# W1's first group loaded through ScalarE's DMA queue, and x's first total moved behind the first fp32 products

## The chip, the cores and the metric

The kernel runs on one core of one Trainium2 chip. A time is the device time of one launch in microseconds (us). The kernel before takes 1239.53 us, the median of 3 runs (1239.34 to 1239.58).

## What is computed

The inputs are x (16 batches, 512 rows, 512 columns, fp32), a list of one expert number for each batch, and the weights of two layers.

```python
h = gelu(einsum('bni,ih->bnh', x, W1) + b1)             # W1: 512 x 2048
shared_x = einsum('bnh,ho->bno', h, W2) + b2            # W2: 2048 x 384
expert_x = einsum('bnh,bhp->bnp', h, We[indices]) + be[indices][:, None, :]   # 128 columns
out = x + concatenate([shared_x, expert_x], axis=-1)
```

The gelu is the exact one. Operands and result are fp32.

## The kernel before

The kernel is written by hand for each engine: every engine runs a fixed list of instructions, and semaphores order them against each other. An fp32 product is made of three fp16 products. Each operand is scaled by a power of two and split into a high part (ScalarE, `hi`) and a low part (VectorE, `lo`); TensorE adds up hi x hi, lo x hi and hi x lo. The power of two comes from the largest absolute value of the operand: VectorE reduces each partition to its maximum, TensorE sums these over the partitions with a matmul against ones (`total`), and VectorE turns the sum into a scale with three small operations (`power`).

The 2048 hidden columns are cut into D = 4 groups (d = 0 to 3) of C = 4 tiles (c = 0 to 3) of 128. Batches 1 to 15 use Strassen-like sums of blocks. Batch 0 is plain, and it has a special start: its group 0 (d = 0) isn't split at all. `first_group` multiplies raw fp32 W1 with raw fp32 x, so that TensorE can begin as soon as the data are there, before any scale is known. Each such product of 128x128 by 128x512 in fp32 shows as two matmul records of the profile. The loops of `first_group` run over the four row blocks k of x (outside) and the four tiles c (inside), each c into a bank of its own, `banks` for c = 0 and 1, `q_ps` for c = 2, `out_ps` for c = 3. Ahead of k = 0 it waits for x's first half and for the first half of W1's group 0; ahead of k = 2 for the second halves, and there it also makes `w1_total(0, 2)`, which waits until VectorE has reduced W1's groups 0 and 1.

What each engine does at the start, in order:

- SyncE issues all loads on its one DMA queue: x's two halves of 512 KB (L356), W1's group 0 in two halves of 512 KB (L360, L361), W1's group 1 (1 MB, L303), b1, W1's groups 2 and 3, and three parts of W2.
- ScalarE loads its activation table, runs a one-column gelu (`gelu_warm`, L622), waits for x's scale, then makes the high parts of x (four `first_x_split`, L412) and of W1's group 1 (L433).
- VectorE sets `ones`; reduces x's four blocks (`first_x_top`, L671: blocks 0 and 1 need x's first half, 2 and 3 the second); makes x's scale (`first_x_scale`, L739 to L681); reduces W1's group 0 (`w1_top(0)`, L671); makes two low parts of x (L685); reduces W1's group 1 (`w1_top(1)`); two more low parts of x; then group 1's scale and so on.
- TensorE runs 36 small matmuls on `ones` (WARM, L1322), then x's total (L1270), which waits for all four of x's reductions, and then `first_group` (L1132). After it come groups 1 to 3 in the split form (L1118 to L1120), starting with `first_layer1(1, 0)`.

The scale of x isn't used by `first_group` itself; it is used by the splits that follow.

Of the kernel before, what the change touches and what calls it, by code (L numbers as in the profile page):

```python
# [19 lines left out]
KC = IN // P  # L20
# [7 lines left out]
BLOCK = KH * 2 * P  # L28
# [43 lines left out]
def build(nc, x, idx, w1, w1f, w2, w2p, we, b1, b2, be, out):  # L72
    with ExitStack() as ctx:
        def sb(name, shape, dt):
            return ctx.enter_context(nc.sbuf_tensor(name, shape, dt))

        def sem(name):
            return ctx.enter_context(nc.semaphore(name))
# [29 lines left out]
        first_x_max = sb("first_x_max", [P, KC], BF16)  # L108
# [29 lines left out]
        w1_tops, w2_tops, first_x_tops = tops[:, 0:D], tops[:, D:2 * D], tops[:, 2 * D:2 * D + KC]  # L138
# [4 lines left out]
        w1_loaded = [sem(f"w1_loaded{d}") for d in range(D)]  # L143
        w1_rest_loaded = sem("w1_rest_loaded")
# [9 lines left out]
        first_x_max_done = sem("first_x_max_done")  # L154
        first_x_all_done = sem("first_x_all_done")
# [60 lines left out]
        def place(r, part):  # L216

            return h_ring[:, r, part].rearrange("p a n -> p (a n)").bitcast(F32)

        def w1_raw(d):  # L220

            if d == 2:
                return x_raw[:, 1].rearrange("p k n -> p (k n)")
            if d == 3:
                return t_sum[:, :, :, :].rearrange("p a k n -> p (a k n)")
            return place(d, 1)
# [25 lines left out]
        def first_bank(n):  # L252

            if n % RING == 3:
                return out_ps[:, 0]
            bank = banks[:, n % RING] if n % RING < 2 else q_ps[:, 2]
            return bank.rearrange("p j n -> p (j n)")
# [39 lines left out]
        def _(sp):  # L297
# [4 lines left out]
            def load_w1(d):  # L302
                sp.dma_start(w1_raw(d), w1[d]).then_inc(w1_loaded[d], 16)  # L303
# [51 lines left out]
            for k in range(2):  # L355
                sp.dma_start(x_raw[:, 0, KH * k:KH * (k + 1)], x[0, :, KH * k:KH * (k + 1)]  # L356
                             ).then_inc(first_x_loaded[k], 16)

            half = 2 * BLOCK
            sp.dma_start(w1_raw(0)[:, :half], w1f[:, :half]).then_inc(w1_loaded[0], 16)  # L360
            sp.dma_start(w1_raw(0)[:, half:], w1f[:, half:]).then_inc(w1_rest_loaded, 16)  # L361
            load_w1(1)
            sp.dma_start(b1_sb[:, :], b1).then_inc(b1_loaded, 16)
            load_w1(2)
# [44 lines left out]
        def _(act):  # L409
# [5 lines left out]
            def x_split(b, par, i):  # L415
                if i in T_OF:
                    act.wait_ge(t_added, 4 * (b - 1) + T_READY[i])

                if isinstance(b, int) and b == 1:
                    act.wait_ge(first_l1_done, HT)  # L420
                else:
                    act.wait_ge(l1_done, OPS * (strassen(b, 0) - 1) + i + 1)
                act.wait_ge(x_scaled, b + 1)
                nc.scalar.activation(x_hi[:, i], x_operand(par, i), ACT.Copy,
                                     scale=scale[:, par, 0:1]).then_inc(x_hi_done, 1)
# [126 lines left out]
            def batch(b, par, last=False, sums=False, w2_s=False):  # L552
# [64 lines left out]
                if isinstance(b, int) and b == 1:  # L617
                    x_split(b + 1, 1 - par, P4)
                    x_split(b + 1, 1 - par, P3)

            act.wait_ge(ones_set, 1)
            nc.scalar.activation(gelu_warm[:, :], ones[:, 0:1], ACT.Gelu)  # L622
            for k in range(KC):
# [491 lines left out]
        def _(pe):  # L1115
# [6 lines left out]
            def first_group():  # L1122

                raw = w1_raw(0).rearrange("p (k c m) -> p k c m", k=KC, c=C)
                for k in range(KC):
                    if k % KH == 0:
                        pe.wait_ge(first_x_loaded[k // KH], 16)
                        pe.wait_ge(w1_loaded[0] if k == 0 else w1_rest_loaded, 16)
                    if k == KH:
                        w1_total(0, 2)  # L1130
                    for c in range(C):
                        last = nc.tensor.matmul(first_bank(c), raw[:, k, c], x_raw[:, 0, k],  # L1132
                                                start=k == 0, stop=k == KC - 1)
                        if k == KC - 1:
                            last.then_inc(first_l1_done, 1)

            def first_layer1(d, c):

                n, i, j = C * d + c, c // 2, c % 2
                if d == 1 and j == 0:  # L1140
                    pe.wait_ge(w1_lo_done, i + 1)
                elif c == 0:
                    pe.wait_ge(w1_lo_done, d + 1)
                pe.wait_ge(first_gelu_done, n - RING + 1)
                for k in range(KC):
                    if n == C:
                        pe.wait_ge(first_x_lo, k + 1)
                    op, kc = A_OP[i][k // KH], k % KH
                    last = product(first_bank(n), w1_hi[:, d, op, kc, j],
                                   w1_lo[:, d, op, kc, j], first_x[0][:, k], first_x[1][:, k], k == 0, k == KC - 1)  # L1150
                last.then_inc(first_l1_done, 1)
# [116 lines left out]
            def total(to, of, start=True):  # L1268

                return nc.tensor.matmul(to, ones[:, :P], of, start=start, stop=True, skip_group_check=True)  # L1270

            def w1_total(a, n):
                pe.wait_ge(w1_max_done, a + n)
                total(w1_tops[:, a:a + n], w_max[:, a:a + n]).then_inc(w1_all_done, n)
# [23 lines left out]
            def first_batch():  # L1298
                first_group()
                for c in range(C):  # L1300
                    first_layer1(1, c)
                    if c == 0:

                        x_total(0)
                        w1_total(2, 2)
                for c in range(C):
                    first_layer1(2, c)
                pe.wait_ge(w2_max_done, D)
                total(w2_tops, w_max[:, D:2 * D]).then_inc(w2_all_done, 1)
                for c in range(C):  # L1310
                    first_layer1(3, c)
                    if c == 1:
                        e_total(0)
                for unit in range(OT * C):
                    layer2(0, 0, unit)
                x_total(1)
                for unit in range(OT * C):
                    layer2(0, 1, unit)

            pe.wait_ge(ones_set, 1)  # L1320
            for _ in range(WARM):
                nc.tensor.matmul(out_ps[:, 1, :N // 2], ones[:, :P], ones[:, :], start=True, stop=True)  # L1322
            pe.wait_ge(first_x_max_done, KC)
            total(first_x_tops, first_x_max[:, :]).then_inc(first_x_all_done, 1)
            first_batch()
            for b in (1, 2):
                for d in range(D):
# [58 lines left out]
```

## Time and profile before

| | us |
|---|---|
| median of 3 runs | 1239.53 |
| the profiled execution, its own time | 1239.52 |
| its span, first to last instruction | 1237.8 |
| TensorE busy | 1232.1 (x9368 matmuls) |
| VectorE busy | 940.0 |
| ScalarE busy | 742.4 |

All times in the rows below count from the start of the span. The span is 1.7 us shorter than the execution's own time; what lies around it isn't in the trace. An engine's idle time in front of an instruction is given in brackets with what released the instruction. A DMA appears twice: as the short instruction that issues it (SPq, SyncE's queue) and as its time from issue to landing. A matmul's end is modelled, so neighbouring matmuls overlap in the rows; the distance between starts is what one costs.

### The profile page before, as it was taken

Reading aid. Unit: us, or ns where it says so; the run is one execution under the profiler, and the core shown is the slowest. Engines: PE = TensorE matmul, PEld = TensorE weight load, DVE = VectorE, ACT = ScalarE, POOL = GpSimd, SP = SyncE. Lnnn points to the kernel's source line nnn. Section 1 sums busy time; section 2 is a strip of 40 time slices with the busy share of each in tenths; the row PEclk is TensorE's granted clock in tenths of the full one; section 3 lists DMA queues with packets and bytes.
Section 4 is the critical chain, followed back from the end, with each engine's and each line's share of the span. In section 5 each row is a group of like instructions: output and inputs, shape, how many; then the busy total and the mean of one; then the engine's idle time right before and its main releaser. Section 6 shows DMA issues by size and latency. Waiting matters only on the chain.

```text
span 1237.8 us, 23794 instructions
## 1 busy us (share of the span) xinstructions
PE 1232.1 (100%) x9368; PEld 917.4 (74%) x9368; DVE 940.0 (76%) x1201; ACT 742.4 (60%) x944; POOL 0.2 (0%) x4
## 2 busy tenths in 40 slices
PE   9999999999999999999999999999999999999998
PEld 4456667787787777777777877778778777777775
DVE  7986677877777877768878688787787777777765
ACT  4656556666566665666566566565666656666553
POOL 0000000000000000000000000000000000000000
PEclk9999999999999999999999999999999999999999
DMA  8223123012020110202002020030300203011000
GB/s 306 69 73 123 43 77 95 1 35 69 0 102 0 54 47 0 102 0 68 34 0 102 0 96 6 0 101 0 102 0 21 81 0 102 0 51 51 1 35 35
DMA packets 25234, 64.45 MB, mean 52 GB/s; under 512 B 5104, under 2 KB 5104, under 8 KB 22000
## 3 DMA queue, kind: packets, MB, share of 16 engines
q1 hardware_dynamic: 25200, 63.99, 15.1%
q8 instruction: 22, 0.36, 0.1%
q14 instruction: 12, 0.10, 0.0%
HBM read 47.20 MB, written 16.78 MB: 52 GB/s over the span
## 4 chain that ended last, share of the span: by engine, by line
PE 99%; DMA 1%; DVE 0%; SPq 0%; issue 0%
PE banks L1118 15%; PE banks L1119 15%; PE banks L1120 15%; PE out_ps L1120 9%; PE out_ps L1119 9%; PE out_ps L1118 9%; PE q_ps L1118 8%; PE q_ps L1119 8%; PE q_ps L1120 8%; PE banks L1132 1%; DMA h_ring<-w1f_dram 1%; PE out_ps L1132 0%; PE q_ps L1132 0%; SPq L356 0%; DVE x_raw L918 0%
## 5 line engine op out<-in xcount | busy, mean ns | idle before, releaser
L1120 PE MATMUL banks<-x_hi,w_lo 128*128 128x256 f16 (+1 forms) x1704 | 467.0, 274 | 0.0
L1119 PE MATMUL banks<-x_lo,w_hi 128*128 128x256 f16 (+1 forms) x1704 | 467.0, 274 | 0.0
L1118 PE MATMUL banks<-x_hi,w_hi 128*128 128x256 f16 (+1 forms) x1704 | 467.0, 274 | 0.0
L685 DVE SCALAR_TENSOR_TENSOR h_ring<-u,scale,h_ring 128x2048 f16<-128x2048 f32 x120 | 281.1, 2343 | 6.9 <-ACT h_ring L450 4.8
L517 ACT ACTIVATE kept<-banks 128x512 f32<-128x512 f32 x180 | 106.3, 591 | 170.3 <-PE banks L1120 170.3
L1118 PEld LDWEIGHTS banks<-x_hi,w_hi 128*128 128x128 f16 x1704 | 166.7, 98 | 44.1 <-ACT kept L517 0.5
L1119 PEld LDWEIGHTS banks<-x_lo,w_hi 128*128 128x128 f16 x1704 | 166.7, 98 | 43.2 <-issue 0.3
L1120 PEld LDWEIGHTS banks<-x_hi,w_lo 128*128 128x128 f16 x1704 | 166.7, 98 | 21.8
L458 ACT ACTIVATE h_ring<-u,scale 128x2048 f16<-128x2048 f32 x56 | 112.1, 2002 | 96.7 <-DVE u L861 96.7
L548 ACT ACTIVATE u<-u,b_sb,undo 128x512 f32<-128x512 f32 x120 | 91.2, 807 | 124.1 <-DVE u L906 124.1
L893 DVE TENSOR_TENSOR u<-banks,kept 128x512 f32<-128x512 f32 x60 | 41.5, 691 | 160.5 <-PE banks L1120 148.9
L450 ACT ACTIVATE h_ring<-u,scale 128x2048 f16<-128x2048 f32 x64 | 127.5, 1992 | 4.4 <-PE out_ps L1120 4.3
L1120 PE MATMUL q_ps<-h_ring,w_sums 128*128 128x256 f16 x448 | 122.1, 273 | 0.0
L1119 PE MATMUL q_ps<-h_ring,w_sums 128*128 128x256 f16 x448 | 122.1, 272 | 0.0
L1118 PE MATMUL q_ps<-h_ring,w_sums 128*128 128x256 f16 x448 | 122.1, 272 | 0.0
L1119 PE MATMUL q_ps<-h_ring,w_hi 128*128 128x256 f16 (+1 forms) x400 | 115.8, 290 | 0.0
L1120 PE MATMUL q_ps<-h_ring,w_lo 128*128 128x256 f16 (+1 forms) x400 | 115.8, 290 | 0.0
L1118 PE MATMUL q_ps<-h_ring,w_hi 128*128 128x256 f16 (+1 forms) x400 | 115.8, 290 | 0.0
L1118 PE MATMUL out_ps<-h_ring,w_hi 128*128 128x512 f16 x256 | 97.0, 379 | 0.0
L1119 PE MATMUL out_ps<-h_ring,w_hi 128*128 128x512 f16 x256 | 97.0, 379 | 0.0
L1120 PE MATMUL out_ps<-h_ring,w_lo 128*128 128x512 f16 x256 | 97.0, 379 | 0.0
L1118 PE MATMUL out_ps<-h_ring,e_hi 128*128 128x512 f16 x256 | 97.0, 379 | 0.0
(142 smaller groups left out, 1664.9 us busy)
## 6 DMA issues: line engine op xcount, KB each, us to landing
e_raw<-we_dram SPq DMA_DIRECT2D x16, 1024.0 KB, 4.7
out_dram<-x_raw SPq DMA_DIRECT2D x64, 256.0 KB, 2.3
x_raw<-x_dram SPq DMA_DIRECT2D x60, 256.0 KB, 3.6
h_ring<-w_dram SPq DMA_DIRECT2D x5, 1024.0 KB, 7.7
t_sum<-w2p_dram SPq DMA_DIRECT2D x2, 1024.0 KB, 4.8
w_sums<-w_dram SPq DMA_DIRECT2D x2, 768.0 KB, 14.4
x_raw<-x_dram SPq DMA_DIRECT2D x2, 512.0 KB, 4.4
h_ring<-w1f_dram SPq DMA_DIRECT2D x2, 512.0 KB, 6.6
```

The costliest lines, as they stand in the source:

```text
L450: nc.scalar.activation(h_ring[:, d % 2, 0, 0], u[:, d % 2].rearrange("p c n -> p (c n)"), ACT.Copy, scale=scale[:, par, 1:2]).then_inc(h_h ...
L458: nc.scalar.activation(h_ring[:, d % 2, 1, 0], u[:, d % 2].rearrange("p c n -> p (c n)"), ACT.Copy, scale=scale[:, par, 1:2]).then_inc(ht_ ...
L517: nc.scalar.activation(kept[:, k], banks[:, BANK_A], ACT.Copy).then_inc(copies_done, 1)
L548: done = nc.scalar.activation(to[:, j], to[:, j], ACT.Gelu, scale=un, bias=b1_sb[:, C * d + j:C * d + j + 1])
L685: return nc.vector.scalar_tensor_tensor(to, of, s, hi, ALU.mult, ALU.subtract)
L893: nc.vector.tensor_tensor(u[:, d % 2, 0:2, :NH], banks[:, BANK_B], kept[:, 0], ALU.add).then_inc(c11_added, 1)
L1118: nc.tensor.matmul(ps, hi, v_hi, start=start, stop=False, skip_group_check=True)
L1119: nc.tensor.matmul(ps, hi, v_lo, start=False, stop=False, skip_group_check=True)
L1120: return nc.tensor.matmul(ps, lo, v_hi, start=False, stop=stop, skip_group_check=True)
L1132: last = nc.tensor.matmul(first_bank(c), raw[:, k, c], x_raw[:, 0, k], start=k == 0, stop=k == KC - 1)
```

## The change

The two loads of W1's group 0 are issued by ScalarE, on ScalarE's own DMA queue, ahead of its activation table and `gelu_warm`. On SyncE's queue W1's group 1 then follows directly behind x. On TensorE the wait for x's four reductions and x's total stand no longer ahead of `first_group`, but inside it, behind the products of k = 0 and c = 2, with the product of c = 3 next.

```diff
@@ sync
             for k in range(2):
                 sp.dma_start(x_raw[:, 0, KH * k:KH * (k + 1)], x[0, :, KH * k:KH * (k + 1)]
                              ).then_inc(first_x_loaded[k], 16)
-
-            half = 2 * BLOCK
-            sp.dma_start(w1_raw(0)[:, :half], w1f[:, :half]).then_inc(w1_loaded[0], 16)
-            sp.dma_start(w1_raw(0)[:, half:], w1f[:, half:]).then_inc(w1_rest_loaded, 16)
             load_w1(1)
@@ scalar
+            half = 2 * BLOCK
+            act.dma_start(w1_raw(0)[:, :half], w1f[:, :half]).then_inc(w1_loaded[0], 16)
+            act.dma_start(w1_raw(0)[:, half:], w1f[:, half:]).then_inc(w1_rest_loaded, 16)
             act.wait_ge(ones_set, 1)
             nc.scalar.activation(gelu_warm[:, :], ones[:, 0:1], ACT.Gelu)
@@ tensor, first_group
                         if k == KC - 1:
                             last.then_inc(first_l1_done, 1)
+                        if k == 0 and c == 2:
+                            pe.wait_ge(first_x_max_done, KC)
+                            total(first_x_tops, first_x_max[:, :]).then_inc(first_x_all_done, 1)
@@ tensor, ahead of first_batch()
-            pe.wait_ge(first_x_max_done, KC)
-            total(first_x_tops, first_x_max[:, :]).then_inc(first_x_all_done, 1)
             first_batch()
```

## Rows read from the trace of the kernel before

**Rows 1.** The page: engines' busy time, and the chain that ended last.
```profile
PE 1232.1 (100%) x9368; PEld 917.4 (74%) x9368; DVE 940.0 (76%) x1201; ACT 742.4 (60%) x944; POOL 0.2 (0%) x4
...
PE 99%; DMA 1%; DVE 0%; SPq 0%; issue 0%
```

**Rows 2.** Waits of TensorE, whole span: who for whom, us, times, longest.
```profile
PE out_ps L1322 <- DVE ones L1051: 1.2, 1, 1.2
PE banks L1132 <- DMA h_ring<-w1f_dram: 0.5, 1, 0.5
PE q_ps L1270 <- DVE first_x_max L671: 0.4, 1, 0.4
```

**Rows 3.** Timeline, loads issued and ScalarE's start: start us, us, what.
```profile
0.73 1.28 ACT L622 ACT_TABLE_LOAD   x1 [0.73 <-PEq L1379]
0.74 0.86 SPq L356 DMA_DIRECT2D x_raw<-x_dram  x2
1.64 0.43 SPq L360 DMA_DIRECT2D h_ring<-w1f_dram  x1
2.03 0.20 ACT L622 ACTIVATE gelu_warm<-ones 128x1 f32<-128x1 bf16 x1
2.12 0.54 SPq L361 DMA_DIRECT2D h_ring<-w1f_dram  x1
2.70 0.53 SPq L303 DMA_DIRECT2D h_ring<-w_dram  x1
```

**Rows 4.** One source line each (L356, L360, L361): issue to landing, first and last issue.
```profile
L356 SPq DMA_DIRECT2D x_raw<-x_dram x2: 381/398/416, 0.7 to 1.2; - x2
DMA to landing us min/median/max: 4.0/4.4/4.8
...
DMA to landing us min/median/max: 6.2/6.2/6.2
...
DMA to landing us min/median/max: 7.0/7.0/7.0
```

**Rows 5.** Timeline of VectorE and ScalarE from x's landing to W1's totals.
```profile
4.72 2.52 DVE L671 TENSOR_REDUCE first_x_max<-x_raw 128x1 bf16<-128x512 f32 x4 [3.59 <-DMA x_raw<-x_dram]
8.08 0.15 DVE L681 TENSOR_SCALAR scale<-inv 128x1 int32<-128x1 int32 x1
8.27 2.56 ACT L412 ACTIVATE x_hi<-x_raw,scale 128x512 f16<-128x512 f32 x4 [6.04 <-DVE scale L681]
9.21 2.29 DVE L671 TENSOR_REDUCE w_max<-h_ring 128x1 bf16<-128x2048 f32 x1 [0.97 <-DMA h_ring<-w1f_dram]
11.41 1.40 DVE L685 SCALAR_TENSOR_TENSOR x_lo<-x_raw,scale,x_hi 128x512 f16<-128x512 f32 x2
12.73 2.28 DVE L671 TENSOR_REDUCE w_max<-h_ring 128x1 bf16<-128x2048 f32 x1
```

**Rows 6.** Timeline of TensorE over the same stretch.
```profile
1.19 5.67 PE L1322 MATMUL out_ps<-ones 128*128 128x256 bf16 x36 [1.19 <-DVE ones L1051]
7.29 0.18 PE L1270 MATMUL q_ps<-first_x_max,ones 128*128 128x4 bf16 x1 [0.44 <-DVE first_x_max L671]
7.97 1.95 PE L1132 MATMUL banks<-x_raw,h_ring 128*128 128x512 f32 x4 [0.50 <-DMA h_ring<-w1f_dram]
14.06 1.02 PE L1132 MATMUL out_ps<-x_raw,h_ring 128*128 128x512 f32 x2
15.16 0.16 PE L1270 MATMUL q_ps<-w_max,ones 128*128 128x2 bf16 x1
15.18 1.10 PE L1132 MATMUL banks<-x_raw,h_ring 128*128 128x512 f32 x2
22.13 0.38 PE L1118 MATMUL banks<-x_hi,w_hi 128*128 128x512 f16 x1
```

**Rows 7.** Windows: length, busy PE PEld DVE ACT POOL, clock, DMA share, GB/s.
```profile
1.75:4.00 2.25, 2.25 (x13) 1.57 (x11) 0.00 (x0) 0.47 (x2) 0.00 (x0) 1.00 0.86 231
4.00:8.00 4.00, 3.06 (x26) 2.39 (x24) 2.94 (x7) 0.00 (x0) 0.00 (x0) 1.00 1.03 394
8.00:12.00 4.00, 4.00 (x10) 1.85 (x11) 3.00 (x4) 2.56 (x4) 0.00 (x0) 1.00 0.99 401
```

**Rows 8.** Windows of L1322 alone (the matmuls on ones); columns length, PE, PEld, clock.
```profile
1.19:4.50 3.31, 3.31 (x16) 2.38 (x17) 1.00 0.74 220
4.50:7.00 2.50, 2.36 (x22) 1.86 (x19) 1.00 1.02 377
```

**Rows 9.** The end: TensorE's last matmul, and windows behind it.
```profile
1234.05 0.27 PE L1120 MATMUL q_ps<-h_ring,w_sums 128*128 128x256 f16 x1
...
1236.00:1236.50 0.50, 0.00 (x0) 0.00 (x0) 0.00 (x0) 0.00 (x0) 0.00 (x0) 1.00 0.67 246
1236.50:1237.00 0.50, 0.00 (x0) 0.00 (x0) 0.00 (x0) 0.00 (x0) 0.00 (x0) 0.63 0.79 295
```

## The prediction

> **What bounds the kernel now.** I read the page first: TensorE is busy in 100% of the span and makes 99% of the chain that ended last [rows 1]. So only two things can move the time: work on TensorE, which the change leaves alone, and holes in TensorE's work. The waits of TensorE show how few there are: 1.2 us for `ones` at the very start, 0.4 us for x's maxima, 0.5 us for W1 [rows 2], nothing later. The change therefore acts only in the first 15 us, and what it wins or loses there goes through to the end unchanged, since from 15.18 us on TensorE runs without a hole. There is one hole more, which the view of waits doesn't name: the last product of k = 1 (a pair of records) starts at 14.06 us, a product is 0.86 us, so the next would start at 14.92, but `w1_total` runs at 15.16 [rows 6]. VectorE had ended `w1_top(1)` at 12.73 + 2.28 = 15.01 [rows 5]. So at this point TensorE waits for VectorE already, by 0.24 us. This is the row that decides the case: the fp32 stage has its second half behind VectorE's list, and an earlier first product doesn't move VectorE.
>
> The 0.86 us is worked out so: seven products lie between the starts at 7.97 and 14.06, 6.09 us or 0.87 each, and eight between 15.18 and 22.13, 6.95 us, again 0.87 [rows 6]; where products follow each other closely it is 0.86.
>
> **The loads.** Landings are issue plus duration [rows 3, 4]: x's halves at 0.74 + 4.0 = 4.7 and 1.2 + 4.8 = 6.0, W1's halves at 1.64 + 6.2 = 7.84 and 2.12 + 7.0 = 9.12. The 2.1 MB run back to back: 231 GB/s from 1.75 to 4 us at a busy share of 0.86, then 394 and 401 GB/s at a share of 1.0 [rows 7]. So after 4 us the 16 engines have no room, and issuing W1 at 0.73 instead of 1.64 makes no byte faster; it only changes whose bytes go first. Before, x had the first 1.05 MB to itself. After, W1 takes part of them.
> - W1's first half goes forward. Shared evenly, it and x's first half are the first 1.05 MB and land near 6.0, where x's second half landed before.
> - x's second half goes back. Its bounds: 6.0 if SyncE's queue is always served first, 9.1 if it is the last of the four. If the queues take turns it ends with W1's second half at 9.1 or a packet ahead. I take 8.7, nearest to that end, 0.4 off for the stretch before 4 us, where a share of 0.86 at 231 GB/s leaves some room for two queues.
>
> The Trainium skill, "DMA: Bandwidth & Descriptors", section "Issuing engines are not separate DMA queues", speaks against the change: both queues run on the same 16 engines and interleave, and a second issuer saves only the time of issuing. The rates in the rows agree with that; by this rule x's second half is at the late end, near 9.1, and the sum below would be 0.4 us larger.
>
> **VectorE.** From x's second landing (L) to `w1_total`, everything is in rows 5 and 6. Two reductions of x: 4 took 2.52, so 2 take 1.26. To the total on TensorE 0.05 (7.24 to 7.29). From there over the three small operations to where `w1_top(0)` could start: 7.29 to about 8.24, 0.95. From the start of `w1_top(0)` over two low parts and `w1_top(1)` to `w1_total`: 9.21 to 15.16, 5.95. Together `w1_total` is at L + 8.21. With the L of before, 6.0, that is 14.2; it was at 15.16 because `w1_top(0)` waited 0.97 us for W1's second half (9.12 + 0.09 + 5.95) [rows 5]. So the old order had a slack of 1 us on x and none on W1. With L = 8.7 `w1_total` is at 16.9, or **1.75 us later** than 15.16. W1's second half then lands at about 9.1 and isn't the one that is waited for (VectorE gets to it at 8.7 + 1.26 + 0.05 + 0.95 = 11.0).
>
> The high parts of x on ScalarE move with the scale and keep their lead over the low parts (8.27 and 0.71 each against 11.41) [rows 5]; nothing else enters.
>
> **TensorE.** The 36 matmuls on `ones` end at 1.19 + 5.67 = 6.86 [rows 6]. Then x's total no longer stands in the way, W1 and x are there at about 6.0 to 6.9, and the fp32 products start at about 6.9 instead of 7.97: 1.1 us gained at this point. Three products (c = 0, 1, 2) take 2.6, to 9.5. Now comes the moved wait: x's maxima are complete at 8.7 + 1.26 = 9.96, so TensorE stands 0.5 us. Behind the wait are queued the product of c = 3 and all of k = 1, five products or 4.3 us, to 14.4. At `w1_total` TensorE waits for VectorE until 16.9, 2.5 us. All of the gain is waited away there, and 1.75 us on top. The total itself is one matmul of 0.18 us in both versions, among the fp32 ones.
>
> The stage behind (k = 2 and 3, then the split products of group 1) starts 1.75 us later, and so do VectorE's and ScalarE's steps that feed it, since they hang on the same chain: relative to each other nothing changes, and no new wait follows.
>
> **Edits at no cost.** ScalarE's two issues, 0.43 and 0.54 us by SyncE's rows, stand ahead of table load 1.28 and `gelu_warm` 0.20 [rows 3], together to about 3.3 us, and ScalarE is next needed at 8.27 after 6.04 us idle [rows 5]; without that cover they would cost 0.97. Does ScalarE issue at 0.73 or behind the table load? The table load started at 0.73, before `ones` was set, so it doesn't head the list by need; I take issue first, and give the other order to a rival. SyncE issues W1's group 1 at 1.6 instead of 2.70 [rows 3]; it stays behind the same bytes, and is needed at `w1_top(1)`, 12.73 before and 14.5 after.
>
> **Sum.** The profiled execution took 1239.52 (span 1237.8, 1.7 around it), its median 1239.53. The sum on that: 1239.5 + 1.75 = **1241.3**.
>
> **Rivals.**
> 1. *x keeps a head start* (ScalarE issues at about 2.0, behind its table load, or its queue gets the smaller share). W1's bytes then begin 1.3 us after x's, by which time about 0.29 MB of x has gone; x lands at about 8.2 and W1's second half at about 9.8: `w1_total` at 8.2 + 8.21 = 16.4, plus 1.25, 1240.8. A still smaller share for W1 doesn't help, since W1's second half then comes so late that its own chain (landing + 6.04) rules. The best split at the same total rate loses over 1 us. In the same rival, a start that two queues fill at the full rate from 2 us on brings all landings 0.7 to 1 us forward: 1240.3 to 1240.6.
> 2. *The clock falls* (the slower side). The rows of the matmuls on `ones` show both levels: 16 in 3.31 us, 0.207 each, at 1.2 GHz, then 22 in 2.36 us, 0.107 each, at 2.4 GHz [rows 8]. The hole from 6.86 to 7.97, with one small matmul in it, cost nothing [rows 6]. At the end the last matmul is over at 1234.3, and the granted clock is full until 1236.5 and 0.63 in the half microsecond behind [rows 9]: it fell after some 2.3 us without work. The hole I expect at `w1_total` is 2.5 us, with 0.5 us of another one 4.3 us ahead: longer than what was survived, as long as what wasn't. If the clock falls there, TensorE runs at half speed for as long as at the start, some 3.2 us, and loses half of it, 1.6 us: 1239.5 + 1.75 + 1.6 = 1242.9. The hole reaches 2.3 us once L + 8.21 is 2.3 behind TensorE's 13.8, so from an L of about 7.9 on; from there it decides.
> 3. *The early start counts in full.* First product at 6.9, no hole behind: minus 1.1 and minus 0.24, 1238.2. TensorE would be at `w1_total` at 6.9 + 6.9 = 13.8, so x would have to land by 13.8 - 8.21 = 5.6 and W1's second half by 13.8 - 6.04 = 7.8: more bytes than the engines moved at full share. Against it are rows 7.
> 4. *Two queues disturb each other*, and x lands beyond 9.5: plus 2.6, 1242.1 or more. No row speaks for it.
>
> **How the numbers follow.** Forecast 0.48, rival 1 0.17, rival 2 0.30, rival 3 0.02, rival 4 0.03. The likeliest alone is 1240.9 (x at 8.3) to 1241.7 (9.1). The range for 8 in 10 takes in rivals 1 and 2: 1240.1 to 1243.3. A measurement of this kernel can tell 0.2%, or 2.5 us, from no change. Forecast and rival 1 are slower by 0.7 to 2.2 us, inside that; rival 2 and rival 4 lie beyond, rival 3 inside. So faster 0.01, same 0.66, slower 0.33.
>
> **What the profile after would show.** First fp32 product near 6.9, with no wait for W1. x's second reduction pair starting near 8.7 with an idle time of VectorE ahead of it. x's total behind three products, near 10.0. `w1_top(0)` with no wait for DMA, near 11.0. `w1_total` near 16.9 and the first split product near 23.9 against 22.13 [rows 6]. The matmuls behind `w1_total` 0.43 us apart, or 0.85 if rival 2 holds. I would be wrong if x's second half landed before 7, or if TensorE had a new wait after 24 us.

## The result, and the profile of the changed kernel

The changed kernel takes 1244.20 us (median of 7 runs, 1242.53 to 1244.36), the kernel before 1239.46 in the same comparison: ratio 1.0034, 95% interval 1.0025 to 1.0043. It is slower by 4.7 us, and the forecast of 1241.3 with its range up to 1243.3 was too low. The runs lie at two levels: five at 1244.2 to 1244.4, two at 1242.53 and 1242.54. The execution shown here is one of the upper five (1244.36, span 1242.6).

The timeline of the changed kernel first; start, duration, engine, line, what, and in brackets the idle time before it. These lines answer to [rows 3, 5, 6].

```profile
0.73 0.41 ACTq L619 DMA_DIRECT2D h_ring<-w1f_dram  x1
0.74 0.86 SPq L356 DMA_DIRECT2D x_raw<-x_dram  x2
1.19 5.96 PE L1325 MATMUL out_ps<-ones 128*128 128x256 bf16 x36 [1.19 <-DVE ones L1051]
...
7.60 1.28 DVE L671 TENSOR_REDUCE first_x_max<-x_raw 128x1 bf16<-128x512 f32 x2 [6.47 <-DMA x_raw<-x_dram]
...
7.89 1.96 PE L1132 MATMUL banks<-x_raw,h_ring 128*128 128x512 f32 x4 [0.74 <-DMA h_ring<-w1f_dram]
...
10.13 1.28 DVE L671 TENSOR_REDUCE first_x_max<-x_raw 128x1 bf16<-128x512 f32 x2 [1.24 <-DMA x_raw<-x_dram]
...
11.47 0.18 PE L1273 MATMUL q_ps<-first_x_max,ones 128*128 128x4 bf16 x1 [0.76 <-DVE first_x_max L671]
...
12.34 2.29 DVE L671 TENSOR_REDUCE w_max<-h_ring 128x1 bf16<-128x2048 f32 x1
...
15.86 2.28 DVE L671 TENSOR_REDUCE w_max<-h_ring 128x1 bf16<-128x2048 f32 x1
...
18.29 0.16 PE L1273 MATMUL q_ps<-w_max,ones 128*128 128x2 bf16 x1 [2.25 <-DVE w_max L671]
...
18.32 3.41 PE L1132 MATMUL banks<-x_raw,h_ring 128*128 128x512 f32 x4
...
26.96 0.38 PE L1118 MATMUL banks<-x_hi,w_hi 128*128 128x512 f16 x1
```

Read it from the end. The first split product starts at 26.96 against 22.13 [rows 6], 4.83 us later, and the span is 4.8 us longer: nothing behind 27 us matters. Of the 4.83, 3.13 are there at `w1_total` (18.29 against 15.16), where TensorE stood 2.25 us for VectorE. The other 1.70 come from the eight fp32 products behind it: from 18.32 to 26.96 is 8.64 us against 6.95 before.

Both have their own row. The 3.13 begin at x's second half: it lands at 10.1 instead of 6.0, and VectorE's chain behind it is the forecast one, 10.1 + 8.21 = 18.3. The 1.70 are the clock. Windows of TensorE in the changed kernel (length, PE busy with its records, granted clock, DMA share, GB/s):

```profile
16.00:18.00 2.00, 0.04 (x1) 1.00 1.01 417
18.00:20.00 2.00, 1.71 (x4) 0.67 1.01 415
20.00:22.00 2.00, 2.00 (x4) 0.50 0.91 375
```

The windows that follow show 0.98 and 1.00. The clock was at half for some 3.4 us, from about 18.7 to 22.1, right behind the hole, and four fp32 records took 3.41 us instead of the 1.95 of [rows 6]. The two runs at 1242.5 are 3.07 us above the kernel before, what the 3.13 alone would give.

Why x landed late shows in the windows of all engines (the last three columns are clock, DMA share and GB/s), to be held against [rows 7], where 4 to 8 us is at 394 GB/s:

```profile
1.75:4.00 2.25, 2.25 (x13) 1.58 (x11) 0.00 (x0) 1.40 (x2) 0.00 (x0) 1.00 0.86 222
4.00:6.00 2.00, 2.00 (x15) 1.60 (x14) 0.00 (x0) 0.00 (x0) 0.00 (x0) 1.00 0.92 221
6.00:8.00 2.00, 1.26 (x12) 0.92 (x10) 0.40 (x1) 0.00 (x0) 0.00 (x0) 1.00 1.00 377
```

The slow start of the transfers, 231 GB/s until 4 us in the kernel before, lasts until 6 us. The first halves of x and W1 landed at 7.6 and 7.7, the second ones at 10.1 and 10.6. Two us at 221 GB/s instead of 394 are 0.35 MB short. At 410 GB/s, about the rate behind it, that is 0.85 us, an estimate that covers more than half of the 1.4 us by which the landing of x was missed.

### The profile page after: what moved, and what is told of

Its sections match the earlier page's. It is cut to its first block, busy times and chain, and to the rows that moved or that the text cites. A ratio compares the mean times of both kernels' runs of the same rounds, so it can differ in the third digit from the quotient of the medians.

```text
span 1242.6 us, 23794 instructions
## 1 busy us (share of the span) xinstructions
PE 1234.2 (99%) x9368; PEld 918.0 (74%) x9368; DVE 940.1 (76%) x1201; ACT 742.3 (60%) x944; POOL 0.2 (0%) x4
## 4 chain that ended last, share of the span: by engine, by line
PE 98%; DVE 1%; DMA 1%; issue 0%; SPq 0%
PE banks L1118 15%; PE banks L1120 15%; PE banks L1119 15%; PE out_ps L1119 9%; PE out_ps L1120 9%; PE out_ps L1118 9%; PE q_ps L1118 8%; PE q_ps L1120 8%; PE q_ps L1119 8%; DMA x_raw<-x_dram 1%; PE banks L1132 0%; DVE w_max L671 0%; PE q_ps L1132 0%; PE out_ps L1132 0%; DVE x_lo L685 0%; DVE first_x_max L671 0%
```

## The experiments

**One part at a time.** The first run has W1 on ScalarE's queue but x's total ahead of the fp32 products, the second the moved total alone.

```diff
 # e1_queue_alone, against the changed kernel
-                        if k == 0 and c == 2:
-                            pe.wait_ge(first_x_max_done, KC)
-                            total(first_x_tops, first_x_max[:, :]).then_inc(first_x_all_done, 1)
 ...
+            pe.wait_ge(first_x_max_done, KC)
+            total(first_x_tops, first_x_max[:, :]).then_inc(first_x_all_done, 1)
             first_batch()
```

> The first part of the change alone: W1's group 0 on ScalarE's queue, x's total in its old place ahead of the fp32 products. The changed kernel had x's second half at 10.1 us instead of 6.0 and w1_total at 18.29 instead of 15.16. Theory 1 (everything hangs on x's second landing L, w1_total = L + 8.21): L about 10.1 again, x's total at L + 1.31 = 11.4, first fp32 product at 11.5, so TensorE reaches w1_total at 11.5 + 6.9 = 18.4, VectorE at 18.3: plus 3.2 us without the clock. The hole from 6.9 to 11.4 is 4.5 us, longer than any survived, so the clock falls in every run and TensorE does part of k = 0 and 1 at 1.2 GHz: another 1.5 to 2 us, 1244.2 to 1244.8 in all. Rival (the moved total is what costs, the queue is harmless): within 0.3 us of the kernel before, 1239.5.

Measured: 1245.58 us (1244.48 to 1245.74), ratio 1.0046 (1.0030 to 1.0063). x's second half at 10.11, x's total at 11.45 behind a hole of 3.56 us, the first fp32 product at 11.55. In this run the windows from 10 to 16 us all show a clock of 0.50, so that k = 0 and 1 end late and `w1_total` is at 21.09, later than VectorE (18.3). Theory 1 holds for the landing. The time is 0.8 us above the upper end of what was expected, because the clock stayed down so long that TensorE's own products became the bound.

> The second part alone: all loads on SyncE's queue as before, x's total behind k = 0, c = 2. Theory 1: landings as before (x 6.0, W1 7.84 and 9.12), first product at 7.97; x's maxima are done at 7.24, but the total is issued only behind three products, 7.97 + 2.6 = 10.55 against 7.29. The scale follows 0.95 later, w1_top(0) starts at 11.5 against 9.21, and w1_total is at 11.5 + 5.95 = 17.45 against 15.16: plus 2.3 us, 1241.8, and 1243.4 in runs in which the clock falls in the hole from 14.9 to 17.45. Rival (x's total is cheap wherever it stands, only the late landing costs): 1239.5.

Measured: 1241.74 us (10 runs: six at 1241.4 to 1241.8, four at 1243.4 to 1243.8), ratio 1.0022 (1.0012 to 1.0031). Its timeline:

```profile
7.89 1.96 PE L1132 MATMUL banks<-x_raw,h_ring 128*128 128x512 f32 x4 [0.68 <-DMA h_ring<-w1f_dram]
...
10.54 0.17 PE L1273 MATMUL q_ps<-first_x_max,ones 128*128 128x4 bf16 x1
...
11.41 2.29 DVE L671 TENSOR_REDUCE w_max<-h_ring 128x1 bf16<-128x2048 f32 x1
...
17.36 0.16 PE L1273 MATMUL q_ps<-w_max,ones 128*128 128x2 bf16 x1 [2.25 <-DVE w_max L671]
```

x's total has no idle time ahead of it: the maxima had been there since 7.4, and the total stood in TensorE's list behind three products. `w1_total` is 2.2 us later. The moved total alone thus costs 2.2 us. The queue alone costs over 3 (an estimate: in e1 the fall of the clock covers it, but x's landing of 10.1 + 8.21 gives 18.3 for VectorE), and both together cost 3.1 (clock aside). They are two floors under the same chain, and the later one counts.

**The clock.** The changed kernel with TensorE's hole filled:

```diff
 # e3_filled_hole, against the changed kernel
                     if k == KH:
+                        for _ in range(22):
+                            nc.tensor.matmul(out_ps[:, 1, :N // 2], ones[:, :P], ones[:, :], start=True, stop=True)
                         w1_total(0, 2)
```

> The changed kernel, with 22 more matmuls on ones (of 0.107 us, 2.35 us in all, into a bank that nobody reads) ahead of w1_total, where TensorE otherwise stands from 15.9 to 18.3 us. They leave the result as it is. If the fall of the clock to 0.5 between 19 and 22 us is what separates the runs at 1244.2 from those at 1242.5, then the clock stays at 1.0, w1_total stays at 18.3 and all runs are at 1242.5, plus 3.1 over the kernel before. Rival (the two levels have another cause, the landing of x differs from run to run): the two levels stay, or all runs stay near 1244.2.

Measured: 1242.58 us, all ten runs between 1242.37 and 1242.71. `w1_total` at 18.19 as before, clock 1.00 throughout, the split products from 25.16. The upper level is gone, and 1.6 us with it. So the clock is the cause of the second level, and the matmuls cost nothing, since TensorE was waiting anyway.

```profile
15.78 2.56 PE L1131 MATMUL out_ps<-ones 128*128 128x256 bf16 x22
...
18.19 0.16 PE L1275 MATMUL q_ps<-w_max,ones 128*128 128x2 bf16 x1
```

**Queue or order.** All four loads on SyncE's queue, in turn:

```diff
 # e4_one_queue_in_turn, against the changed kernel (the two act.dma_start lines removed)
+            half = 2 * BLOCK
             for k in range(2):
                 sp.dma_start(x_raw[:, 0, KH * k:KH * (k + 1)], x[0, :, KH * k:KH * (k + 1)]
                              ).then_inc(first_x_loaded[k], 16)
+                sp.dma_start(w1_raw(0)[:, half * k:half * (k + 1)], w1f[:, half * k:half * (k + 1)]
+                             ).then_inc(w1_rest_loaded if k else w1_loaded[0], 16)
```

> The changed kernel, but all four loads on SyncE's queue in turn: x first half, W1 first half, x second half, W1 second half. It tells the queue from the order of the bytes. In the changed kernel the 16 engines moved 222 GB/s not only from 1.75 to 4 us but until 6.2 us, which put x's second half at 10.1 instead of the 8.7 expected. Theory Q (a second queue lengthens the slow start of the transfers): here the slow stretch ends at 4 us as before, W1's first half lands at 6.0, x's second at 7.8; first product at 6.9, x's total at 9.5 behind three products, w1_total at 9.5 + 0.95 + 5.95 = 16.4: plus 1.25 us, 1240.7 (1242.3 where the clock falls). Theory O (reading x and W1 in turn is slow by itself): slow until about 6 us, x's second half at 9 or later, w1_total at 17.2 or later, plus 2 us or more.

Measured: 1243.07 us (seven runs; six between 1242.6 and 1243.4, one at 1241.23), ratio 1.0026 (1.0015 to 1.0038).

```profile
1.75:4.00 2.25, 2.25 (x13) 1.57 (x11) 0.00 (x0) 0.47 (x2) 0.00 (x0) 1.00 0.82 248
4.00:6.00 2.00, 2.00 (x11) 1.44 (x10) 1.19 (x2) 0.00 (x0) 0.00 (x0) 1.00 0.88 242
```

One queue, and still 242 GB/s from 4 to 6 us: the order makes the slow stretch, not the second queue. W1's first half landed at 7.3, x's second at 8.55. Theory O holds for the rate, but it set x's landing at 9 or later, and its landing of 8.55 alone would put `w1_total` at 16.76. TensorE set the later floor: W1's first half came at 7.3, the 36 matmuls on `ones` took 6.95 us here instead of the 5.67 of [rows 6], and the first fp32 product was at 7.97. So x's total, three products behind, was at 10.55, when the maxima had been ready at 9.83, and `w1_total` came at 17.37, the same floor as in e2. The converse test uses both queues but deals the halves out so that both read x first:

```diff
 # e6_same_tensor_on_both: SyncE's queue has x's first and W1's first half, ScalarE's the second halves
 ...
+            sp.dma_start(x_raw[:, 0, :KH], x[0, :, :KH]).then_inc(first_x_loaded[0], 16)
+            half = 2 * BLOCK
+            sp.dma_start(w1_raw(0)[:, :half], w1f[:, :half]).then_inc(w1_loaded[0], 16)
 ...
-            act.dma_start(w1_raw(0)[:, :half], w1f[:, :half]).then_inc(w1_loaded[0], 16)
+            act.dma_start(x_raw[:, 0, KH:], x[0, :, KH:]).then_inc(first_x_loaded[1], 16)
```

> The changed kernel with the halves dealt out otherwise: SyncE's queue has x's first half and W1's first half, ScalarE's queue has x's second half and W1's second half. Two queues run, but both read x first and then both read W1. Landings tell why the transfers were slow (222 GB/s) until 6 us in the changed kernel and until 6 us with one queue in turn (242), but only until 4 us in the kernel before. Theory Q (two queues at once are slow): rates near 220 until 6 us again and the last of the four at 10.6 us. Theory O (the first bytes of each tensor are slow to read, and they come early one behind the other when W1 is next to x's first half): 390 GB/s from 4 to 6 us while x's second half moves, x complete near 6 us, the last of the four at 9.1 to 9.8 us.

Measured (one execution, 1243.86 us with the clock fallen):

```profile
1.75:4.00 2.25, 2.25 (x13) 1.57 (x11) 0.00 (x0) 1.40 (x2) 0.00 (x0) 1.00 0.78 266
4.00:6.00 2.00, 2.00 (x16) 1.64 (x15) 0.35 (x1) 0.00 (x0) 0.00 (x0) 1.00 1.04 422
6.00:8.00 2.00, 1.08 (x10) 0.72 (x8) 2.00 (x4) 0.00 (x0) 0.00 (x0) 1.00 1.07 442
```

x complete at 5.8, all four loads at 8.9, a little sooner than in the kernel before. Two queues at once are not slow. At full share they bring little either: 422 and 442 GB/s here, against 406 and 436 in the windows from 6 to 10 us of e4 with one queue, and all four loads 0.2 us earlier than before. The Trainium skill, "DMA: Bandwidth & Descriptors", section "Issuing engines are not separate DMA queues", says that DMAs run on the same 16 engines whoever issues them. These rates agree with that.

**Why the order is slow.** First, whether it is the first read of W1's memory. One run adds a small load of 64 bytes of each of W1's rows on the other queue, ahead of e4's loads:

> The four loads in turn on SyncE's one queue (as in the run with one queue), plus a small load on ScalarE's queue, first of all, of 64 bytes of every 8 KB row of W1's group 0, into a tile that nobody reads. Theory O in the form that the first touch of W1's memory is slow: the small load takes the slow touches on itself, W1's first half lands at 6.0 to 6.6 us instead of 7.3, and the rate from 4 to 6 us is near 390 GB/s instead of 242. If the slow stretch is instead a property of alternating between the tensors on the queue, W1's first half stays at 7.3 us. Whole time within 0.5 us of the run with one queue (1243.1, or 1241.3 where the clock holds), since TensorE starts behind its matmuls on ones anyway.

Measured (one execution): 192 GB/s from 4 to 6 us, W1's first half at 7.7, the whole at 1243.32. It rules nothing out, since the small load itself landed only at 5.4, too late to go ahead of anything. The next two change what the second load reads. They leave W1's group 0 out of batch 0, so that only their landings and rates count:

```diff
 # e8_same_bytes_twice (e9_second_batch_for_w1: x[1, ...] in its place), against e4_one_queue_in_turn
-                sp.dma_start(w1_raw(0)[:, half * k:half * (k + 1)], w1f[:, half * k:half * (k + 1)]
-                             ).then_inc(w1_rest_loaded if k else w1_loaded[0], 16)
+                sp.dma_start(w1_raw(0)[:, half * k:half * (k + 1)].rearrange("p (k n) -> p k n", k=KH),
+                             x[0, :, KH * k:KH * (k + 1)]).then_inc(w1_rest_loaded if k else w1_loaded[0], 16)
```

> One queue in turn, as in the run before it, but the two loads of W1's group 0 read x's first batch instead of W1, each the same bytes as the x load ahead of it. W1's group 0 is thus left out of batch 0 (its place holds x's values). It asks whether the second load is slow because its memory is read for the first time, or because of its place in the order. Theory F (first read of a stretch of memory): the second load reads what was just read, so it takes 1.25 us behind the first and lands near 6.0 (7.3 in the run with W1), and the rate from 4 to 6 us is near 390 GB/s. Theory P (place: any second load of 4 KB pieces behind x's first half is slow): 7.3 us and about 240 GB/s again.

> The same, but the two loads of W1's group 0 read the halves of x's second batch: the same input tensor, a stretch of memory 1 MB further on that nothing has read before. W1's group 0 is left out of batch 0 here too. Theory F (first read of a stretch of memory is slow, whichever tensor it belongs to): the second load lands near 7.3 us and the rate from 4 to 6 us is about 240 GB/s, as with W1. Theory T (it is the change of tensor that is slow): 6.0 us and 390 GB/s.

Measured (one execution each, 1241.28 and 1241.32 us): 246 GB/s from 4 to 6 us with the same bytes twice, 231 with the second batch; the second load landed at 7.3 and 7.4. A load of bytes that have just been read is as slow as W1. So it is neither the first read nor the change of tensor. What is left is that the pieces are 4 KB of rows of 8 KB, and that a lower half follows a lower half. Two orders of the four loads tell that from its neighbours:

```diff
 # e11_other_half_of_w1 on SyncE's queue (e12_second_halves_first: x 1, W1 1, x 0, W1 0)
+            sp.dma_start(x_raw[:, 0, 0 * KH:1 * KH], x[0, :, 0 * KH:1 * KH]).then_inc(first_x_loaded[0], 16)
+            sp.dma_start(w1_raw(0)[:, 1 * half:2 * half], w1f[:, 1 * half:2 * half]
+                         ).then_inc(w1_rest_loaded, 16)
+            sp.dma_start(x_raw[:, 0, 1 * KH:2 * KH], x[0, :, 1 * KH:2 * KH]).then_inc(first_x_loaded[1], 16)
+            sp.dma_start(w1_raw(0)[:, 0 * half:1 * half], w1f[:, 0 * half:1 * half]
+                         ).then_inc(w1_loaded[0], 16)
```

> One queue, in the order x first half, W1 second half, x second half, W1 first half. In memory the two halves are the lower and the upper 4 KB of rows of 8 KB. Slow so far (below 250 GB/s from 4 to 6 us) were all orders in which two lower halves come first, even of the same bytes; fast (356 to 422) were those in which x's lower and upper half come first. Theory H (reading lower halves behind lower halves is slow, because such pieces lie 8 KB apart and the other 4 KB of each row isn't read near them): with W1's upper half as the second load the rate from 4 to 6 us is near 390 GB/s, and it lands near 6.0 us. Theory R (the load that is fast is only one that completes the rows just read, x's second half behind x's first): near 240 GB/s and 7.3 us again. TensorE's start is later here, since W1's first half comes last; the whole time isn't the point.

> One queue, in the order x second half, W1 second half, x first half, W1 first half: two upper halves first, then two lower ones. Theory H: slow from 4 to 6 us as with two lower halves, about 240 GB/s, second load at 7.3 us. If it is the lower half alone that is slow to read: 390 GB/s from 4 to 6 us, and the slow stretch comes later or not at all. Theory R says about 240 GB/s too; this run and the one before it together tell the three apart.

Measured, e11 first (x lower, W1 upper, x upper, W1 lower):

```profile
4.00:6.00 2.00, 2.00 (x20) 1.77 (x19) 1.27 (x2) 0.00 (x0) 0.00 (x0) 1.00 1.05 369
6.00:8.00 2.00, 0.69 (x7) 0.38 (x4) 0.01 (x1) 0.00 (x0) 0.00 (x0) 1.00 0.91 268
```

and e12 (upper, upper, lower, lower):

```profile
4.00:6.00 2.00, 2.00 (x18) 1.72 (x17) 0.00 (x0) 0.00 (x0) 0.00 (x0) 1.00 0.93 227
```

With W1's upper half behind x's lower one the second load is fast (it landed at 6.0), though it comes from another tensor and completes no row: theory R falls. The slow stretch then comes later, from 6 to 8 us, where an upper half stands behind an upper half. In e12 two upper halves are as slow as two lower ones. The whole times, 1247.2 and 1247.1 (one execution each), are those of a kernel whose first fp32 product waits for the last load, with the clock fallen behind the wait.

But "the same half one behind the other is slow" isn't the whole rule, as the second pairs of loads show. In e4 W1's upper half follows x's upper half, in e12 W1's lower half follows x's lower one, and both pairs ran at full rate:

```profile
6.00:8.00 2.00, 2.00 (x16) 1.58 (x15) 0.09 (x1) 0.00 (x0) 0.00 (x0) 1.00 1.01 406
8.00:10.00 2.00, 2.00 (x7) 0.93 (x6) 1.28 (x2) 0.00 (x0) 0.00 (x0) 1.00 1.07 436
...
6.00:8.00 2.00, 0.86 (x8) 0.52 (x6) 0.00 (x0) 0.00 (x0) 0.00 (x0) 1.00 0.98 387
8.00:10.00 2.00, 0.00 (x0) 0.00 (x0) 1.29 (x3) 0.00 (x0) 0.00 (x0) 1.00 1.04 424
```

The first two lines are e4's, the others e12's. What is shown is that the first two loads are slow when they read the same half, and that in e11 a same-half pair was slow in the second and third place. Why the later pairs of e4 and e12 weren't stays open.

The layout itself can be tried too. In the next run the changed kernel reads each half from a place where it lies in one piece.

```diff
 # e13_halves_packed, against the changed kernel
-                sp.dma_start(x_raw[:, 0, KH * k:KH * (k + 1)], x[0, :, KH * k:KH * (k + 1)]
+                sp.dma_start(x_raw[:, 0, KH * k:KH * (k + 1)], x0[k]
 ...
+        "x0": np.asarray(x)[0].reshape(N, 2, KH, P).transpose(1, 3, 2, 0),
 ...
-        "w1f": w1f.reshape(P, 4 * BLOCK),
+        "w1f": w1f.reshape(P, 2, 2 * BLOCK).transpose(1, 0, 2),
 ...
```

> The changed kernel, two queues, with each half of W1's group 0 and of x's first batch stored by itself in memory (a second copy of x's first batch as an input), so that each load reads 512 KB in one piece instead of 4 KB of every 8 KB. Theory H: the slow stretch ends near 4 us, the rate from 4 to 6 us is near 390 GB/s, x's second half lands at 8.5 to 8.9 as the prediction had it, w1_total is at 16.7 to 17.1, and the whole is 1241.1 to 1241.5, or 1.7 more where the clock falls. Theory R or any that has nothing to do with how the halves lie in memory: 222 GB/s, x at 10.1, w1_total at 18.3, 1242.5 or 1244.2 as the changed kernel.

Measured: 1241.37 us (ten runs; seven between 1240.6 and 1241.5, three between 1242.5 and 1243.3), ratio 1.0017 (1.0007 to 1.0026).

```profile
1.75:4.00 2.25, 2.25 (x13) 1.57 (x11) 0.00 (x0) 1.40 (x2) 0.00 (x0) 1.00 0.91 313
4.00:6.00 2.00, 2.00 (x16) 1.61 (x15) 0.51 (x1) 0.00 (x0) 0.00 (x0) 1.00 1.04 418
...
6.96 1.88 PE L1132 MATMUL banks<-x_raw,h_ring 128*128 128x512 f32 x4
7.97 1.28 DVE L671 TENSOR_REDUCE first_x_max<-x_raw 128x1 bf16<-128x512 f32 x2 [1.19 <-DMA x_raw<-x_dram]
...
9.54 0.17 PE L1273 MATMUL q_ps<-first_x_max,ones 128*128 128x4 bf16 x1
...
16.36 0.16 PE L1273 MATMUL q_ps<-w_max,ones 128*128 128x2 bf16 x1 [2.25 <-DVE w_max L671]
```

The slow stretch is gone, and x's second half lands at 7.95 instead of 10.1. That is earlier than the 8.5 to 8.9 that were expected, since the rate until 4 us rose too, from 222 to 313 GB/s. `w1_total` at 16.36 is 9.54 (x's total) + 6.82; by x's landing alone it would be 7.95 + 8.21 = 16.16. So what remains, 1.20 us over the kernel before, is the floor of the moved total. The profiled execution took 1240.73 us, the kernel before plus these 1.2. That the median of 1241.37 is close to the 1241.3 forecast for the changed kernel is therefore partly luck. The layout of the pieces, in the order that the change gives them, is enough to account for the missed landing. How the memory or the DMA engines make such pieces slow isn't shown: the rates say only that 512 KB in 4 KB pieces 8 KB apart ran at 192 to 246 GB/s at this point of the kernel when the load ahead read the same half of its rows. The Trainium skill, "DMA: Bandwidth & Descriptors", section "Latency and other measured facts", lists slow row pitches from 512 KiB up; 8 KB isn't among them, so here the measurement stands alone.

**How far the loss reaches.** Two runs loosen TensorE's waits in the changed kernel, with the loads as changed.

```diff
 # e5_w1_total_behind, against the changed kernel; e10_both_totals_behind has the second edit too
-                    if k == KH:
-                        w1_total(0, 2)
 ...
+                        if k == 2 and c == 1:
+                            w1_total(0, 2)
 # in first_layer1, e10_both_totals_behind alone (taken from behind c = 0 of group 1)
+                    if d == 1 and c == 1 and k == 1:
+                        x_total(0)
+                        w1_total(2, 2)
```

> The changed kernel, with w1_total(0, 2) moved from ahead of k = 2 to behind k = 2, c = 1, so that TensorE has two products (1.7 us) to do while VectorE finishes. The loads and the place of x's total stay as changed. Theory 1 (VectorE's chain from x's landing is what costs, TensorE's hole only shows it): VectorE ends w1_top(1) at 18.2 as before; TensorE reaches the total at 15.9 + 1.7 = 17.6 and stands 0.7 us instead of 2.3, so the clock holds; the low part of W1's group 1 is ready 5.15 us behind the total (15.16 to 20.3 in the kernel before), at 23.5, where TensorE is with its fp32 products too (18.3 + 6 products, 5.2 us = 23.5), against 22.13: plus 1.4 us, 1240.9 in all runs. Rival (the fp32 stage's loss comes from the loads themselves, W1's second half being late for k = 2): w1_total's move changes nothing, 1242.5 or more.

Measured: 1242.55 us (1242.3 to 1242.7), no better than e3. The first split product was at 23.43, as expected, and then a wait that the kernel before doesn't have. Waits of TensorE in this run (who for whom, us, times, longest):

```profile
PE q_ps L1273 <- DVE x_max L693: 1.4, 1, 1.4
...
PE q_ps L1273 <- DVE w_max L671: 0.5, 1, 0.5
```

VectorE's list was 3 us late as a whole, and TensorE met it again at the next total. That total was moved too:

> The changed kernel with w1_total(0, 2) behind k = 2, c = 1, as in the run that gained nothing, and also the next pair of totals (x_total(0) and w1_total(2, 2)) moved from behind tile c = 0 of group 1 to behind k = 1 of tile c = 1. The run before showed the first split product at 23.43 us, as expected, and then a new wait of 1.4 us at the next pair of totals, for VectorE's x_max. Theory 1b (the loss is VectorE's list being 3.1 us late, and it shows at whichever total TensorE meets first without slack): with this total half a tile and more further back, the total is issued near 27.5 us as before, TensorE doesn't stand there, the low part of W1's group 2 is ready at 33.5 and TensorE gets to it at 33.9: 1240.9, plus 1.4 us. Rival (VectorE's delay of 3.1 us must reach TensorE somewhere, since it has no slack behind): 1242.5 again, with the wait at the next place.

Measured: 1241.20 us (1240.92 to 1241.36, all ten runs), ratio 1.0013 (1.0003 to 1.0022), without the wait for `x_max`. Half of the loss of 3.1 us (clock aside) is given back by moving three small matmuls (the three totals in the two edits); of the 1.54 us left, 1.26 are TensorE's own late end of the fp32 products (first split product at 23.39 against 22.13). Theory 1b holds, the rival falls.

**A version that beats both?** The kernel before with `w1_total(0, 2)` behind k = 2, c = 0 (g1), and the same with packed halves (g2):

> The kernel before, with only w1_total(0, 2) moved to behind k = 2, c = 0. Theory 1: TensorE goes on at 14.92 instead of 15.18, the total is at 15.8 instead of 15.16, the low part of W1's group 1 is ready at 20.9, still ahead of the end of the fp32 products at 21.8 to 21.9: minus 0.25 to 0.4 us, 1239.2. Rival (the hole of 0.24 us worked out from the starts at 14.06 and 15.18 isn't real): no change, 1239.5.

> The kernel before (one queue, x's total ahead of the fp32 products), with the halves of x's first batch and of W1's group 0 packed in memory, and w1_total(0, 2) behind k = 2, c = 0. If the layout is the cause of the slow stretch, it also slowed the kernel before, by about 1 us (231 GB/s until 4 us, and W1's first half 1.86 us behind x's second instead of 1.25). Then x lands at 4.5 and 5.7, W1 at 6.9 and 8.1, the first fp32 product is at 7.0, w1_top(0) at 8.2, w1_total possible at 14.15 and issued at 14.8, and TensorE ends the fp32 products near 20.8 instead of 22.1: 1238.4 to 1238.7, minus 1 us against the kernel before. Rival (the layout only matters where two tensors alternate): 1239.3 as with the moved total alone.

Measured: g1 1239.40 against 1239.62 (ratio 0.9998, 0.9989 to 1.0007), g2 1239.43 against 1239.50 (0.9999, 0.9990 to 1.0008). Both beat the changed kernel, but neither can be told from the kernel before, so the expected gain of 1 us in g2 didn't come. In g1's timeline the total goes in at 15.91 without a hole ahead of it, so the 0.24 us of that hole can be taken, but they are too small to be seen in the time. In g2 the rate until 4 us rose from 231 to 342 GB/s and x landed at 4.1 and 5.3, 0.7 earlier; but W1's halves came at 7.84 and 9.1, as in the kernel before, and TensorE's hole ahead of the first fp32 product only grew, from 0.5 to 1.1 us. My gain of 1 us took it that W1 would follow x by 1.25 us each. What holds W1's landing in that order stays open.

## Why the prediction was wrong

1. **What bounds the kernel**: right. All of the change is in the first 27 us, and the deciding row is VectorE's `w1_top(1)`, not TensorE's first product. In e13 TensorE did start at 6.96, 1 us earlier than before, and `w1_total` was still 1.20 us later.
2. **The landing of x's second half**: the step that failed. 8.7 us was forecast between bounds of 6.0 and 9.1; it was 10.1, outside the bounds. The upper bound held the total rate fixed, on the ground that after 4 us the engines are full. The slow stretch until 4 us was taken as a fixed time from the start of the transfers, but with two first halves of rows in front it lasted until 6. e13 shows the cause: with it gone the landing is at 7.95. With the measured landing the prediction's own sum comes out: 10.1 + 8.21 is 3.1 us behind 15.16, and 1239.5 + 3.1 + 1.6 for the clock is 1244.2.
3. **VectorE's chain**: right to 0.1 us, as long as x's total waits for the landing. L + 8.21 gives 18.3 for the measured L; 18.29 was measured.
4. **TensorE's start, and the moved total**: first product 7.89 instead of 6.9, since W1's first half came at 7.7 in the same slow stretch. The end of the matmuls on `ones` isn't fixed either: their slow ones, 0.207 us each in [rows 8], were more in some executions than in others (5.67 us in all in the kernel before, 5.96 in the changed one, 6.95 in e4), and one row was read as if it were the rule. A term was left out as well: x's total stands behind three products, so it can't run before the first product plus 2.6 us, however early x lands, and `w1_total` is 6.82 to 6.9 us behind it. From 7.9 that is 17.4, 2.2 us above the kernel before, as in e2. Even from the hoped-for 6.9 it is 16.4, or 1240.7. The fastest execution of e13, 1240.58, is at this floor. Rival 3, in which the early start counts in full, and the 1240.3 to 1240.6 in rival 1 lie below it.
5. **The clock**: the mechanism was the second rival, and its size of 1.6 us was right (1.70 in the profile, 1.6 from the two levels, 1.6 in e3). Its chance of 0.30 was low: by their times the clock fell in five of seven runs here, and in 18 of 34 of the four kernels with this hole and several runs (the changed one, e2, e4, e13). The condition that the prediction gave, an x landing later than about 7.9, was wrong. TensorE has five products to do behind x's total, VectorE needs 6.82 us, and the hole of 2.25 us follows from these two alone: it is in e6 with x at 5.8, in e2 at 6.1, in e13 at 7.95 and in the changed kernel at 10.1. The row that warned of it, the end of the kernel before, had an idle time of 2.3 us.
6. **"No new wait follows"**: right for the changed kernel itself, but for a weaker reason than I gave. TensorE and VectorE are late together; as soon as TensorE is less late than VectorE, as in e5, the next total makes it wait 1.4 us.
7. **The range** ended at 1243.3, which is the upper bound of the landing and the clock's 1.6 us together: 1239.5 + 2.2 + 1.6. What lay beyond was the landing, outside its own bounds. The range thus had room for the clock on top of an x at 9.1, and not for both it and 10.1. The prediction also took 2.5 us as the least that a measurement can tell from no change. The interval of the ratio, 1.0025 to 1.0043, tells about half of that.

## What to carry to other kernels

Before a load is brought forward, find who waits for the load that it pushes back: here W1's loads, which were brought forward, had held up TensorE by 0.5 us and VectorE by 0.97, while x's second half had about 1 us of slack and was pushed back by 4.1, which leaves the 3.1 us that were lost. A small matmul that starts a chain on other engines belongs as early in TensorE's list as its data allow; behind three products it cost 2.2 us, though TensorE itself lost nothing there. And a hole of over 2 us on TensorE that can't be removed is better filled with work that nobody reads. Left open, the one of 2.25 us cost the products behind it about 1.6 us more in about half of the runs; filled, it cost them nothing in ten of ten.

## What the runs showed of the hardware that was not expected

- Loads of 512 KB, made of 4 KB out of each row of 8 KB, at the start of the kernel: when the first two read the same half of their rows 192 to 246 GB/s from 4 to 6 us (ten kernels, the changed one among them, one or two queues, also with the same bytes twice), when they read different halves 356 to 422 GB/s (five kernels, the one before among them), packed in one piece 373 and 418 GB/s (g2, e13). Later pairs of the same half ran at 406 and 436 GB/s (e4) and 387 and 424 (e12), but at 268 in e11, so the rule behind it is not known.
- The granted clock fell at holes of 2.25 us in 5 of 7 executions of the changed kernel, 4 of 10 of e2, 6 of 7 of e4 and 3 of 10 of e13 by their times. In the profiled ones the windows show it too for the changed kernel, e2, e4, e6 and e7, and a clock of 1.00 throughout for e8, e9 and e13 with the same hole. In e4 it fell inside the hole, in the changed kernel 0.4 us and in e2 about 1.4 us behind its end. It fell behind a hole of 3.56 us in e1, whose four runs all lie at 1244.5 or above, and didn't fall behind holes of 0.5 to 1.4 us (e5, ten executions). Once fallen it stayed at 0.50 for some 3.4 us of work in the changed kernel and from 10 to 16 us in e1, where part of that was hole.
- A DMA issue took ScalarE 0.41 and 0.45 us, about what it takes SyncE (0.43 to 0.54 for the same loads in [rows 3]), and the activation table's load went in behind the two issues, at 1.66 us.
